# All four units of scores in one run, and Wo's product between the next round's flips

## What is computed

```
x = x + L0_xattn(ctx, layernorm(x), mask)   # 8 heads of 64
x = x + L0_ffn(layernorm(x))                # quantised to int8, one 128x128 product
x = x + L1_xattn(layernorm(x), ctx)         # softmax over the tokens
x = x + L1_ffn(layernorm(x))                # the best of 8 experts by router
```

```
q = heads(latents @ Wq);  k, v = heads(concat([ctx, latents]) @ Wkv)   # after layer norms
q = l2norm(q) * q_scale;  k = l2norm(k) * k_scale
attn = softmax(where(mask, q @ k.T * 8, -inf))                        # keys: 77 of ctx, 128 of x
x = x + layer_norm((attn @ v) @ Wo)
```

## Time and profile before

| | |
|---|---|
| time of three runs | 970.62, 973.37, 974.88 us; median 973.37 |
| profiled execution, span from first to last instruction | 950.6 us (its whole time is not given apart from the runs') |
| TensorE, VectorE, ScalarE, GpSimd busy | 912.8, 744.9, 693.5, 458.1 us |
| the chain that ended last | TensorE 69%, VectorE 14%, ScalarE 8% |

### The profile page before, as it was taken

The page is one execution under the profiler, slowest core; times in us unless marked ns, Lnnn a source line. Parts: engine busy times, 40 slices in busy tenths (PEclk is TensorE's granted clock), DMA queues, the critical chain, the costliest instruction groups (busy, mean ns, idle before and its releaser), DMA issues.

```text
span 950.6 us, 30821 instructions
## 1 busy us (share of the span) xinstructions
PE 912.8 (96%) x11286; PEld 794.5 (84%) x11286; DVE 744.9 (78%) x2526; ACT 693.5 (73%) x1671; POOL 458.1 (48%) x1094
## 2 busy tenths in 40 slices
PE   7999999999999999999999999999999999899997
PEld 6788888788878887888788878888888878898997
DVE  5566787888888888888888888888888978877553
ACT  4877777677778787778777777777778766676664
POOL 5422433354535453545354444444454545777554
PEclk9999999999999999999999999999999999999999
DMA  7743000000000000000000000000000022245310
GB/s 196 200 124 57 2 2 2 2 13 2 14 2 14 2 14 2 13 3 10 5 10 5 8 8 8 7 8 7 8 8 8 7 47 71 61 97 106 95 55 20
DMA packets 45193, 31.44 MB, mean 33 GB/s; under 512 B 11555, under 2 KB 40166, under 8 KB 45046
## 3 DMA queue, kind: packets, MB, share of 16 engines
q1 hardware_dynamic: 39398, 19.93, 9.2%
q0 software_dynamic: 4320, 8.50, 2.8%
q10 hardware_dynamic: 1328, 1.06, 0.4%
HBM read 17.75 MB, written 12.17 MB: 31 GB/s over the span
## 4 chain that ended last, share of the span: by engine, by line
PE 69%; DVE 14%; ACT 8%; issue 3%; POOL 3%; DMA 1%; SPq 1%; DVEq 0%; POOLq 0%; ACTq 0%
PE ps L1670 9%; PE ps L1717 9%; PE ps L1643 7%; PE ps L1765 6%; PE ps L1450 5%; PE ps L1622 5%; PE ps L1630 5%; PE ps L1452 5%; PE ps L1451 5%; DVE sumsq L1267 4%; PE ps L1722 3%; ACT probs L604 2%; PE ps L1749 2%; ACT qk_hat L617 2%; PE ps L1496 1%
## 5 line engine op out<-in xcount | busy, mean ns | idle before, releaser
L1374 DVE TENSOR_TENSOR qk_hat<-ps,rstd 128x512 f32<-128x512 f32 x168 | 106.3, 684 | 49.2 <-POOL rstd L870 49.1
L1267 DVE TENSOR_REDUCE sumsq<-qk_hat 128x8 f32<-128x512 f32 x168 | 107.8, 677 | 35.9 <-ACT qk_hat L617 34.7
L863 POOL TENSOR_TENSOR rs_t<-rs_y 128x32 f32<-128x32 f32 x73 | 17.9, 245 | 235.2 <-ACT rs_y L658 235.2
L1670 PE MATMUL ps<-v_x,prob 128*64 128x65 f32 x2048 | 127.9, 225 | 2.1 <-ACT w_all L568 0.4
L1670 PE MATMUL ps<-v_c,prob 128*64 128x65 f32 x2048 | 124.2, 222 | 0.0
L677 ACT ACTIVATE prob<-ps,neg_shift 128x512 f32<-128x512 f32 x128 | 88.4, 690 | 48.6 <-PE ps L1717 48.6
L1670 PEld LDWEIGHTS ps<-v_x,prob 128*64 128x64 f32 x2048 | 105.0, 137 | 20.9 <-issue 19.2
L617 ACT ACTIVATE qk_hat<-ps 128x512 f32<-128x512 f32 x168 | 98.5, 599 | 31.7 <-PE ps L1452 25.8
L1450 PE MATMUL ps<-w_hi,xc_hi 128*128 128x512 f32 x272 | 120.8, 444 | 0.8 <-POOL xc_lo L835 0.8
L1717 PE MATMUL ps<-qT_all,kT_all 64*128 64x128 f32 x1536 | 111.6, 285 | 2.3 <-ACT prob L677 1.1
L1452 PE MATMUL ps<-w_hi,xc_lo 128*128 128x512 f32 x272 | 107.3, 395 | 0.0
(11 more groups left out here) (245 smaller groups left out, 2257.2 us busy)
## 6 DMA issues: line engine op xcount, KB each, us to landing
x_res<-sorted_rows SPq DMA_DIRECT2D x71, 65.5 KB, 1.9
w_all<-in_L_ffn_W_dram SPq DMA_DIRECT2D x16, 256.0 KB, 5.3
sorted_rows<-fill SPq DMA_DIRECT2D x8, 327.5 KB
out_dram<-prob,x_res POOLq DMA_INDIRECT x71
sorted_rows<-stage,idx POOLq DMA_INDIRECT x64, 2.4
ctx_res<-in_ctx_dram SPq DMA_DIRECT2D x8, 115.5 KB
x_res<-in_x_dram SPq DMA_DIRECT2D x1, 768.0 KB
sorted_rows<-fill SPq DMA_DIRECT2D x1, 524.0 KB, 5.0
```

The lines of the kernel that those rows point to most:

```text
L1267: nc.vector.reduce_sum(sumsq[:, n * H:(n + 1) * H], sq[:, n * INNER:(n + 1) * INNER].rearrange("p (h d) -> p h d", d=DH), AX).then_inc(ss_ ...
L1374: nc.vector.tensor_tensor(qk_hat[:, n * INNER:(n + 1) * INNER].rearrange("p (h d) -> p h d", d=DH), ps_qk[:, n, :].rearrange("p (h d) -> p ...
L1670: last = nc.tensor.matmul(dst[half:half + DH, :], prob[:, kt, col + half:col + half + DH], v, start=kt == 0, stop=kt == 1)
```

## The change

Scores 1 follow scores 0 directly: unit 3 is written to bank 3 instead of bank 6, so that all four units have a bank of their own, and scores 1 wait for o_n instead of for the exp of unit 0. The transposes of outputs come behind scores 1, in bank 6, after that exp, and the transposes of tokens behind them. Wo's product goes into the next round, between the flips of k and those of the context keys. Scores of units 0 and 1 are split by keys wherever those of units 2 and 3 are. `slot_a`, which uses bank 3, now waits for the exp of unit 3. On ScalarE the exp of unit 1 goes ahead of o_t, and o_t ahead of xc_t.

```diff
-        ps_v, ps_ot = (ps[:, 6, :], ps[:, 5, :]), ps[:, 3, :]
-        ps_s = (ps[:, 6, :], ps[:, 5, :], ps[:, 4, :], ps[:, 6, :])
+        ps_v = (ps[:, 6, :], ps[:, 5, :])
+        ps_s = (ps[:, 6, :], ps[:, 5, :], ps[:, 4, :], ps[:, 3, :])
...
+        def ps_ot(j, inside):
+
+            return ps[:, 6 if has(j, inside) else 3, :]
...
+                if has(j, inside):
+                    exps((1,))
+                if has(j - 1, inside) and not tail(j, inside):
+                    outputs_copied()
                 if inside or j != -2:
                     scaled_tokens()
-                if has(j - 1, inside) and not tail(j, inside):
-                    outputs_copied()
                 if has(j, inside):
-                    exps((1, 3, 2))
+                    exps((3, 2))
...
             def slot_a(j, rho, g, inside):
 
+                if has(j - 1, inside):
+                    pe.wait_ge(exp_done, 4 * j - 1)
...
             def run(j, par, rho, g, inside, pos, turn):
+                def flipped(n):
+                    pe.wait_ge(scaled, 3 * j + 1 + n)
...
                 if has(j, inside):
...
+                    flipped(0)
+                    flipped(1)
+                if has(j - 2, inside):
+
+                    pe.wait_ge(ot_done, j - 1)
+                    if not has(j + 1, inside) and has(j - 3, inside):
+                        pe.wait_ge(o_cent, j - 2)
+                    if has(j + 1, inside):
+                        pe.wait_ge(xct_sb, j + 2)
+                    for t in range(PAIRS):
+                        last = nc.tensor.matmul(ps_o, o_t[:, t * P:(t + 1) * P], wo_sb[:, t, :],
+                                                start=t == 0, stop=t == PAIRS - 1)
+                    last.then_inc(wo_done, 1)
+                if has(j, inside) and fresh(pos):
+                    flipped(2)
                 slot_a(j, rho, g, inside)
...
-                            if kt == 0 or halves(pos)[0] == halves(pos)[1]:
+                            if same:
...
                     scores(0)
+                if has(j - 1, inside):
+                    pe.wait_ge(on_done, j)
+                elif has(j, inside):
+                    pe.wait_ge(s["w_copied"], 6)
+                if has(j, inside):
+                    scores(1)
+                if has(j - 1, inside):
+
+                    if has(j, inside):
+                        pe.wait_ge(exp_done, 4 * j + 1)
+                    for t in range(PAIRS):
+                        last = nc.tensor.transpose(ps_ot(j, inside)[:, t * P:(t + 1) * P], o_n[:, t * P:(t + 1) * P], ident[:, :])
+                    last.then_inc(onT_done, 1)
                 seven_emptied(j, rho, g, inside)
...
-                if has(j, inside):
-
-                    pe.wait_ge(exp_done, 4 * j + 1)
-                    if halves(pos)[0] != halves(pos)[1]:
-                        pe.sem_inc(s["fence_t"], 1)
-                    scores(1)
```

More of the change, by code:

```diff
@@ L1637, in run @@
             def run(j, par, rho, g, inside, pos, turn):
-                if has(j, inside):
-                    for n in range(3) if fresh(pos) else range(2):
-                        pe.wait_ge(scaled, 3 * j + 1 + n)
-                        for t in range(PAIRS):
-                            last = nc.tensor.transpose(ps_qk[:, n, t * P:(t + 1) * P],
-                                                       qk_hat[:, n * INNER + t * P:n * INNER + (t + 1) * P], ident[:, :])
-                        last.then_inc(qkT_done, 1 if n == 0 or fresh(pos) else 2)
+                def flipped(n):
+                    pe.wait_ge(scaled, 3 * j + 1 + n)
+                    for t in range(PAIRS):
+                        last = nc.tensor.transpose(ps_qk[:, n, t * P:(t + 1) * P],
+                                                   qk_hat[:, n * INNER + t * P:n * INNER + (t + 1) * P], ident[:, :])
+                    last.then_inc(qkT_done, 1 if n == 0 or fresh(pos) else 2)
+                if has(j, inside):
+                    flipped(0)
[12 more added lines that the diff above has]
+                    flipped(2)
                 slot_a(j, rho, g, inside)
@@ L1709, in scores @@
                 def scores(kt):
+                    same = halves(pos)[0] == halves(pos)[1]
                     for t in range(PAIRS):
@@ L1744, in run @@
                     last.then_inc(xcT_done, 1)
-                if has(j - 1, inside):
-                    pe.wait_ge(on_done, j)
-                    for t in range(PAIRS):
-                        last = nc.tensor.transpose(ps_ot[:, t * P:(t + 1) * P], o_n[:, t * P:(t + 1) * P], ident[:, :])
-                    last.then_inc(onT_done, 1)
-                if has(j, inside):
-                    pe.wait_ge(exp_done, 4 * j + 1)
-                    if halves(pos)[0] != halves(pos)[1]:
-                        pe.sem_inc(s["fence_t"], 1)
-                    scores(1)
-                if has(j - 1, inside):
-                    pe.wait_ge(ot_done, j)
-                    if not has(j + 2, inside) and has(j - 2, inside):
-                        pe.wait_ge(o_cent, j - 1)
-                    if has(j + 2, inside):
-                        pe.wait_ge(xct_sb, j + 3)
-                    for t in range(PAIRS):
-                        last = nc.tensor.matmul(ps_o, o_t[:, t * P:(t + 1) * P], wo_sb[:, t, :],
-                                                start=t == 0, stop=t == PAIRS - 1)
-                    last.then_inc(wo_done, 1)
             def keep_busy(n):
```

5 lines of the change are left out of this document (3 added, 2 removed).

## The result

The changed kernel takes 995.13 us, median of 4 runs (993.48 to 998.61); the kernel before, on the same chip, 972.62 (970.62 to 974.88). The ratio is 1.0224, 95% interval 1.0195 to 1.0252: slower by 22.5 us, in the predicted range of 970 to 998, and 7 us above the forecast of 988.

What follows compares the result with a forecast made beforehand. The prediction took TensorE's queue order and its waits as the bound. Its terms added 1.90 us to a 96.44 us lap, +15 over eight laps; span 966 plus 22.8 gave 988 us, range 970 to 998.

Steps and rivals of the forecast that it cites:

- (a): Scores 1 wait for VectorE's o_n, which frees bank 3: they start at S0+1.11, not 0.95.
- late round: One of two rounds of eight, those of the second attention's exps, where VectorE delivers o_n, q and k late.
- (b): Wo's product waits for o_t, then xc_t: starts at S0+3.85, not 3.63; -0.04 us in two rounds of eight.
- (c): Rounds with two xc_t: Wo's product starts at S0+4.20; +0.20 us, in three rounds of eight this alone.
- router's round: Fourth round with two xc_t, where ScalarE's delay also makes TensorE wait for lg_t: +0.38 us.
- one-token rounds: Rounds with a single xc_t copy ahead of Wo's product: two of eight, -0.04 us each.
- two-token rounds: Rounds with two xc_t because a context block comes in two rounds later; three have only this, +0.20 us each.
- (d): In two rounds of eight the flips wait for VectorE's late q and k, with Wo's product behind them: +0.50 us each.
- For what lies around the span: Step from profiled span to run time: the median lies 22.8 us above the span, carried from 966 to 988.
- the drains decide: Rival, faster: ScalarE delivers o_t and xc_t before TensorE's eight flips end, so mode changes saved count; about 963 us, chance 0.14.
- It cancels: Rival, same: places where TensorE already waits for VectorE absorb the delays; lap +0.3 us, 976 us, chance 0.16.
- ScalarE did not become the bound: Rival, slower by more: ScalarE's later exps delay the chain to rstd; lap +3.4 us, 1000 us, chance 0.10.

Runs made afterwards that it cites:

- tokens_first: Changed kernel with the tokens' transposes ahead of the outputs' and ScalarE's xc_t ahead of o_t: 987.46 us, ratio 1.0139 to the kernel before.
- tokens_early: Changed kernel with the tokens' transposes ahead of the scores and xc_t ahead of the exps, except in the late rounds: 974.20 us, ratio 0.9987 to before.
- wo_alone: Kernel before with only Wo's product moved, between the flips of q and k and those of context keys: 980.87 us, ratio 1.0062.
- wo_split: Kernel before with Wo's product moved as in wo_alone, but ahead of all flips in the two late rounds: 974.81 us, ratio 1.0000.
- early_rounded: tokens_early plus, in late rounds, ScalarE's Ln and Exp ahead of copies v_s, and q_round between o_n and scaled q, k: 961.01 us, ratio 0.9871 to before.

## Why the prediction was right, and where it was off

**(a)** Right. In the round of S0 417.54 o_n ends at 418.59, S0+1.05, scores 1 start 0.06 behind it, and the outputs' transposes begin at S0+2.20 as worked out; in the late round scores 1 begin at 1.66 (1.67 predicted), waiting for o_n.

**(b), (c)** The mechanism was right: tokens_first and tokens_early move the two copies and the transposes that feed them, nothing else, and the loss of these six rounds goes with them. The size was too small. Wo was put at 3.85 and 4.20 and came at 3.98 and 4.35. Of the 0.13, o_t was 0.04 late and xc_t another 0.02; the rest is the step "starts 0.06 after an xc_t ends": it is 0.14 (421.38 to 421.52). The number of semaphores is not the reason. Wo's product waits for o_t and xc_t in the kernel before too, and there, where o_t comes last (here in the router's round, o_t's end at 420.04), it starts 0.06 behind it:

```profile
419.44 0.60 ACT L698 ACTIVATE o_t<-ps 128x512 f32<-128x512 f32 x1
```

```profile
420.10 1.16 PE L1765 MATMUL ps<-wo_sb,o_t 128*128 128x128 f32 x8
```

In tokens_first, where o_t comes last again, it is 0.07. What differs is which of the two comes last. The trace has the wait for xc_t as a record of its own in TensorE's queue, ahead of the product. In the kernel before it runs from 419.60 to 419.65 (L1763), long passed when o_t is there. In the change xc_t comes last, the record stands between, and the step is 0.14 or 0.15 without exception: in the round of S0 440.98 xc_t ends at 445.18, the record (L1662) runs from 445.22 to 445.27, and the first weights load at 445.30:

```profile
445.30 0.86 PEld L1664 LDWEIGHTS ps<-wo_sb,o_t 128*128 128x128 f32 x7 [0.59 <-issue]
```

The prediction had taken its 0.06 from a wait behind whose end no such record stood. The one-token rounds came at +0.05 each instead of -0.04, three two-token rounds at +0.34 instead of +0.20.

**The round of the router.** +0.40 against +0.38, by the two parts named, though neither has the size that it was given. In the round of S0 429.39 the slot comes at S0+5.33 instead of 5.08, +0.25 against +0.20 for the two xc_t, and lg_t's transpose at 6.57, not 6.67:

```profile
435.96 0.33 PE L1524 MATMUL ps<-ident,lg_t 128*128 128x128 f32 x1
```

So this sum fits better than its terms do.

**(d)** Right: +0.57 and +0.52 against +0.50, q's flips at S0+3.74 as worked out, the slot at 6.16 against 6.10. wo_alone and wo_split isolate it.

**The sum.** A lap grew by 2.65 us, not 1.90. By terms: the one-token rounds are 0.18 above the prediction together, the three two-token rounds 0.42, the router's round 0.02, the late ones 0.09, in all 0.71 of the 0.75. Eight laps make +21 instead of +15, and the measured time grew by 22.5. Lap and time lie just above the upper bound of 2.6 and +21, which moreover I had reached by other terms (a start from a standstill in the late rounds, and a delay of VectorE). The range of the time held; the term that was mis-sized is the way from scores 1 to Wo in (b) and (c), above all the step from xc_t's end to Wo, 0.08 of the 0.13 a round.

**"For what lies around the span."** This step was wrong: 1.8 us lie around it, and of the 22.8, 20.4 were the short last part of one execution (174.5 against 194.9). It cancels in a difference, so it did no harm to the forecast. And the reading "0.059 between scores" is a mean: the sixteen records start in eight pairs, 0.11 us apart, the second pair 0.21 behind the first, so that a run pays both at its start (0.10) and at its end (0.09).

**The rivals.** That the drains decide failed as a forecast, on the condition that I had set for it: the chain to the end of xc_t is longer than the cover. The gain itself is real and shows as soon as the chain is taken away: 1.99 us for the run (tokens_early) against 2.04 worked out (0.95 + 1.09) and 2.18 for two. The trace thus agrees with the Trainium skill's rule (TensorEngine Tiling (Array Packing), Key Properties) that changing the tiling mode drains TensorE, as far as an interruption costs 0.19 us in the scores; whether something else at the two ends of a run makes up part of this time was not tested. "It cancels" fell with the waits, and ScalarE did not become the bound: it is busy 73.2 us of the lap, as before.

## What to carry to other kernels

When work is gathered into an unbroken run, list what it used to cover: here the copies of two groups of transposes, which had been made under the second half of the scores, became the last thing that the next product waited for, and a saving put at 0.5 us a round turned into a loss of 0.3. Ask of each buffer that two products share whose copy must come first, and make that copy ahead of the run, not behind it. And when an operation is moved on VectorE, look at what GpSimd does at the new place, and at what is queued behind it: four roundings of 0.87 us took 2.0 in one place, and in another 0.87 that held up no flip.

## What the runs showed of the hardware

TensorE began 0.05 to 0.07 us behind the end of what it waited for (442.53 to 442.59; 420.04 to 420.10 in the kernel before; 511.45 to 511.52 in tokens_first), the last two with two semaphores to wait for, and 0.14 to 0.15 where the last thing awaited was that of a record of its own in the queue (421.38 to 421.52, 445.18 to 445.33). The run of scores takes 1.99 us to the next group on tiles of 64x128 (tokens_early, 428.10 to 430.09) and 1.91 on tiles of 64x64 with twice the records (453.10 to 455.01 there), both without a wait: the split costs nothing, it gains 0.08. The 2.14 of early_rounded's late round (435.47 to 437.61, tiles of 64x64) hold a wait for o_n, which ends at 436.52, S0+1.05; so do the 2.20 of the change. One rounding on VectorE took 1.2 instead of 0.28 us beside an operation of GpSimd and ended 0.08 us behind it. And one program's executions differed by 20 us in their last 190 us alone, in which TensorE's granted clock fell for stretches to 1.2 GHz, while the rounds repeated to 0.1 us a lap; a lap in the steady part is therefore the sharper measure of a change than the time of a run.
